# Turning the second norms of batches 1 to 3 by VectorE blocks and memory, in place of TensorE transposes

## What is computed

```
x = x + attention(layernorm(x))     # per batch: 16 heads, gated slot attention with 64 slots
x = x + ffn(layernorm(x))           # the "second norm"
ffn(n) = ((silu(n @ fp8(gate_w) * gate_s) * (n @ fp8(up_w) * up_s)) @ fp8(down_w)) * down_s
```

## Time and profile before

| | |
|---|---|
| median of 3 runs | 1351.48 us (1348.45 to 1352.53) |
| profiled execution, its own time | 1351.25 us |
| its span | 1349.5 us |
| TensorE (PE) busy | 1323.1 us, 98% of the span |
| VectorE (DVE) busy | 1054.4 us, 78% |
| ScalarE (ACT) busy | 426.6 us, 32% |
| granted TensorE clock | 1.00 over the span |
| attention up to the first feed-forward-only step | 0 to about 1097 us |
| feed-forward steps | about 1097 to 1349.5 us |

### The profile page before, as it was taken

How to read it: one execution, slowest core, us unless ns; L and a number is a source line. 1 busy time by engine, 2 the same in 40 slices (tenths; PEclk the granted TensorE clock), 3 DMA queues, 4 the chain that set the end, 5 groups by cost and what they waited for, 6 DMA issues and landing times.

```text
span 1349.5 us, 24276 instructions
## 1 busy us (share of the span) xinstructions
PE 1323.1 (98%) x9287; PEld 1096.6 (81%) x9287; DVE 1054.4 (78%) x1675; ACT 426.6 (32%) x1283; POOL 137.9 (10%) x106
## 2 busy tenths in 40 slices
PE   6999999999999999999999999999999999999998
PEld 5788888788888888888788788878888878888887
DVE  8888888888888888888888888888778875535354
ACT  4333323332333233233323332333333333222221
POOL 3001101110120012001100110111110010000000
PEclk9999999999999999999999999999999999999999
DMA  6147555655665575556655665565333430000000
GB/s 187 40 106 167 123 121 127 163 114 116 147 135 121 115 167 126 126 117 156 132 132 121 152 133 119 118 158 124 87 92 84 124 109 0 32 1 31 0 32 32
DMA packets 500559, 144.58 MB, mean 107 GB/s; under 512 B 359648, under 2 KB 491616, under 8 KB 500448
## 3 DMA queue, kind: packets, MB, share of 16 engines
q1 hardware_dynamic: 500448, 143.08, 45.5%
HBM read 85.80 MB, written 57.21 MB: 106 GB/s over the span
## 4 chain that ended last, share of the span: by engine, by line
PE 78%; DVE 9%; SPq 5%; DMA 4%; issue 2%; ACT 1%; POOL 0%; DVEq 0%
PE bank L486 15%; PE bank L488 14%; PE bank L487 14%; PE bank L118 13%; PE bank L1659 6%; PE bank L726 3%; SPq L369 3%; PE bank L709 2%; PE bank L566 2%; PE bank L546 2%; DMA fp_weights<-q 2%; SPq L334 2%; DMA e_tokens<-k_tok_then_wT 1%; PE bank L645 1%; PE bank L714 1%
## 5 line engine op out<-in xcount | busy, mean ns | idle before, releaser
L486 PE MATMUL bank<-wvg_hi,xT_hi 128*128 128x512 f32 x512 | 206.6, 404 | 0.7
L488 PE MATMUL bank<-wvg_hi,xT_lo 128*128 128x512 f32 x512 | 199.9, 390 | 0.0
L487 PE MATMUL bank<-wvg_lo,xT_hi 128*128 128x512 f32 x512 | 199.7, 390 | 0.0
L786 ACT ACTIVATE a_and_v<-bank 128x256 f32<-128x256 f32 x128 | 49.2, 384 | 326.8 <-PE bank L488 326.8
L486 PEld LDWEIGHTS bank<-wvg_hi,xT_hi 128*128 128x128 f32 x512 | 96.2, 188 | 25.5 <-issue 4.2
L488 PEld LDWEIGHTS bank<-wvg_hi,xT_lo 128*128 128x128 f32 x512 | 96.1, 188 | 20.5
L487 PEld LDWEIGHTS bank<-wvg_lo,xT_hi 128*128 128x128 f32 x512 | 96.3, 188 | 17.8
L1103 DVE RECIPROCAL cT<-cT 128x512 f32<-128x512 f32 x32 | 107.0, 3342 | 0.0
L1048 POOL TENSOR_TENSOR rstd<-ssq,neg_half 128x8 f32<-128x8 f32 x32 | 52.4, 1638 | 490.9 <-DVE ssq L1151 490.9
L486 PE MATMUL bank<-wo_hi,oT_hi 128*128 128x512 f32 x256 | 99.8, 390 | 0.0
L488 PE MATMUL bank<-wo_hi,oT_lo 128*128 128x512 f32 x256 | 99.6, 389 | 0.0
(11 more groups left out here) (168 smaller groups left out, 3036.9 us busy)
## 6 DMA issues: line engine op xcount, KB each, us to landing
o_transposed<-o SPq DMA_DIRECT2D x27, 512.0 KB, 3.4
oT_lo<-o_transposed SPq DMA_DIRECT2D x108, 128.0 KB, 3.0
fp_weights<-q SPq DMA_DIRECT2D x28, 318.0 KB, 3.2
e_tokens<-k_tok_then_wT SPq DMA_DIRECT2D x31, 256.0 KB, 2.3
e_tok<-e_tokens SPq DMA_DIRECT2D x124, 64.0 KB, 2.3
c_tokens<-cT SPq DMA_DIRECT2D x31, 256.0 KB, 2.4
cT<-c_tokens SPq DMA_DIRECT2D x124, 64.0 KB, 2.3
w_slots<-p SPq DMA_DIRECT2D x27, 256.0 KB, 2.4
```

What stands on the lines that cost most here:

```text
L486: pe.matmul(dst, w_hi, m_hi, start=(k == 0), stop=False)
L487: pe.matmul(dst, w_hi, m_lo, start=False, stop=False)
L488: last = pe.matmul(dst, w_lo, m_hi, start=False, stop=(k == n - 1))
L786: return act.activation(dst, src, ACT.Copy)
```

## The change

Batch 0's second norm stays as it was, in unit 29. Batch 1 joins the late ones (LATE = 3, 12 token tiles t = 0 to 11). Its statistics are taken in unit 30 by the late helpers, those of batch 2 in unit 31, those of batch 3 in steps 2 and 3 of batch 1. TensorE no longer turns any late tile. Instead VectorE normalises tile t into half t % 2 of a double buffer, turns its 32x32 blocks in place (late_turn), SyncE stores the tile to DRAM and loads the previous one with the blocks in their places into the other half of the buffer (store_turned, load_turned), ScalarE rounds it into xT_hi and VectorE takes the remainder, both reading SBUF. Tiles 0 to 7 (batches 1 and 2) go through steps 2 to 11 of batch 0; tiles 8 to 11 (batch 3) through steps 4 to 10 of batch 1, after the results of batch 0 have been stored, since they share the buffer. TensorE waits for xT_lo only at step 10 of a batch, ahead of the next batch's first gate product. ScalarE's and VectorE's code for batch 1 is written out, outside of the loop.

```diff
@@ -649 +649 @@
                 if tail and i >= 2:
-                    pe.wait_ge(s_nl, CH * (i - 1))
+                    pe.wait_ge(s_nl, CH)
...
@@ -730 +730 @@
                 return
-            if tail:
-                norm_transposes(i - 1, (0, 1))
+            if tail and i == 1:
+                norm_transposes(0, (0, 1))
             job(VG3, nu, ni)
-            if tail:
-                pe.wait_ge(s_nl, CH * (i - 1) + 2)
-                norm_transposes(i - 1, (2, 3))
+            if tail and i == 1:
+                pe.wait_ge(s_nl, 2)
+                norm_transposes(0, (2, 3))
...
@@ -894 +894 @@
                 copy(e_tok[:, :, :].rearrange("p c m -> p (c m)"), T1[:, :]).then_inc(s_etok, 1)
-            if tail and i >= 2:
-                norm_hi(i - 2, (2, 3))
+            if tail and i == 2:
+                norm_hi(0, (2, 3))
...
@@ -947 +947 @@
             head_squares(u, 0)
-            if tail and not last:
-                norm_hi(i - 1, (0, 1))
+            if tail and i == 1:
+                norm_hi(0, (0, 1))
...
@@ -1063 +1063 @@
             unit((PAIRS - 1) * B + i, i, last=(i == B - 1), tail=True)
-            if i + 1 < B:
-                norm_rsqrt(i - 1, B + i)
+            if i == 1:
+                norm_rsqrt(0, B + 1)
...
@@ -1254 +1254 @@
             nu, ni = u + 1, i + 1
-            if tail and i >= 2:
-                norm_lo(i - 2, (2, 3))
+            if tail and i == 2:
+                norm_lo(0, (2, 3))
...
@@ -1313 +1313 @@
                 add_y(v, 3)
-            if tail and not last:
-                norm_statistics(i - 1)
+            if tail and i == 1:
+                norm_statistics(0)
+            if tail and i == 2:
+                ffn.late_statistics(dve, 0, range(CH))
+                ffn.late_aggregate(dve, 0)
...
@@ -1325 +1328 @@
                 ffn.times_gate(dve, 0, 1)
-                ffn.late_statistics(dve, 0, (0, 1))
+                ffn.late_statistics(dve, 1, (0, 1))
...
@@ -1334 +1337 @@
             c_turn(nu)
-            if tail:
-                norm_tokens(i - 1, (0, 1))
+            if tail and i == 1:
+                norm_tokens(0, (0, 1))
...
             times_gate(u, i, 0)
-            if tail:
-                norm_lo(i - 1, (0, 1))
-                norm_tokens(i - 1, (2, 3))
+            if tail and i == 1:
+                norm_lo(0, (0, 1))
+                norm_tokens(0, (2, 3))
...
@@ -1405 +1408 @@
         mean_square(UNITS - 1)
-        ffn.late_statistics(dve, 0, (2, 3))
-        ffn.late_aggregate(dve, 0)
+        ffn.late_statistics(dve, 1, (2, 3))
+        ffn.late_aggregate(dve, 1)
...
@@ -1421 +1424 @@
 DOWN_GROUPS = ((0, 4), (4, 5), (5, 6), (6, 7), (7, 11), (11, 12))
-LATE = 2
+LATE = 3
...
@@ -1440 +1443 @@
         self.s_var, self.s_sd = sem("late_var_ready"), sem("late_sd_ready")
-        self.s_xn, self.s_xtr = sem("n3_ready"), sem("n3_transposed")
+        self.s_xn, self.s_xb = sem("n3_ready"), sem("n3_blocks_turned")
+        self.s_xst = [sem(f"n3_blocks_stored{n}") for n in range(2)]
+        self.s_xld = [sem(f"n3T_loaded{n}") for n in range(2)]
+        self.n_dram = nc.dram_tensor("second_norms", (LATE * CH, KT, P, P), F32, kind="Internal").ap()
...
@@ -1564 +1570 @@
         tokens(B - 1, last=True)
+    def turned(t):
+        return ffn.xn[:, 2 + t % 2, :].rearrange("p (k t) -> p k t", k=KT)
+    def late_columns(t):
+        at = (B - LATE) * CH + t
+        return slice(at * P, (at + 1) * P)
...
@@ -1625 +1640 @@
         load_down(4)
-        with sp.Fori(0, B) as b:
+        def store_turned(t):
+            sp.wait_ge(ffn.s_xb, t + 1)
+            sp.dma_start(ffn.n_dram[t].rearrange("k p f -> p k f"), ffn.xn[:, t % 2, :].rearrange("p (k f) -> p k f", f=P)
+                         ).then_inc(ffn.s_xst[t % 2], 16)
+        def load_turned(t):
+            sp.wait_ge(ffn.s_xst[t % 2], 16 * (t // 2 + 1))
+            if t >= 2:
+                sp.wait_ge(ffn.s_xl, t - 1)
+            if t >= 2 * CH:
+                sp.wait_ge(ffn.s_out, 16 * CH)
+            for n in range(BL):
+                rows = slice(BK * n, BK * (n + 1))
+                sp.dma_start(ffn.xn[rows, 2 + t % 2, :].rearrange("t (n m) -> t n m", m=BK),
+                             ffn.n_dram[t].rearrange("k (i t) f -> t (k i) f", t=BK)[:, :, rows]
+                             ).then_inc(ffn.s_xld[t % 2], 16)
+        def late_moves(tiles):
+            for t in tiles:
+                store_turned(t)
+                if t > tiles[0]:
+                    load_turned(t - 1)
+            load_turned(tiles[-1])
+        def store_out(b):
...
                              .rearrange("a p d -> (a p) d"), ffn.res[:, c, :]).then_inc(ffn.s_out, 16)
+        late_moves(range(0, 2 * CH))
+        store_out(0)
+        late_moves(range(2 * CH, LATE * CH))
+        with sp.Fori(1, B) as b:
+            store_out(b)
...
     def _(pe):
-        def late_transposes(t, f):
-
-            pe.wait_ge(ffn.s_xn, t + 1)
-            pe.wait_ge(ffn.s_fu, f - 1)
-            for k in range(KT):
-                mm = pe.transpose(ffn.up_bank(f)[:, k * P:(k + 1) * P], ffn.xn[:, t % CH, k * P:(k + 1) * P],
-                                  ffn.ident[:, :])
-            mm.then_inc(ffn.s_xtr, 1)
-
...
@@ -1681 +1717 @@
                     continue
-                late = first and 2 <= f < 2 + LATE * CH
-                if late:
-                    late_transposes(f - 2, f + 2)
+                if f == FT - 2 and not last:
+                    pe.wait_ge(ffn.s_xl, CH if first else LATE * CH)
...
                     ffn.gate_product(pe, b + 1, f + 2 - FT)
-                if late:
-                    pe.wait_ge(ffn.s_xl, f - 1)
...
@@ -1708 +1741 @@
     def _(act):
-        def late_hi(t, f):
-            act.wait_ge(ffn.s_xtr, t + 1)
-            at = (B - LATE) * CH + t
-            act.activation(ffn.xh[:, :, at * P:(at + 1) * P],
-                           ffn.up_bank(f)[:, :].rearrange("p (k t) -> p k t", k=KT), ACT.Copy).then_inc(ffn.s_xh, 1)
-
-        def tokens(b, first=False, last=False):
-            for f in range(FT):
-                if first and f < 4:
-                    continue
+        def late_hi(t):
+            act.wait_ge(ffn.s_xld[t % 2], 16 * BL * (t // 2 + 1))
+            act.activation(ffn.xh[:, :, late_columns(t)], turned(t), ACT.Copy).then_inc(ffn.s_xh, 1)
+        def tokens(b, first=False, second=False):
+            for f in range(4 if first else 0, FT):
...
                 ffn.fuse_hi(act, b, f)
-                if first and f < 3 + LATE * CH:
-                    late_hi(f - 3, f + 1)
+                if first:
+                    late_hi(f - 4)
+                if second and f >= 6 and f < 6 + CH:
+                    late_hi(2 * CH + f - 6)
...
         ffn.fuse_hi(act, 0, 3)
-        late_hi(0, 4)
-        blocks(act, tokens)
+        tokens(0, first=True)
+        tokens(1, second=True)
+        with act.Fori(2, B) as b:
+            tokens(b)
...
@@ -1743 +1776 @@
                 dve.wait_ge(w["out_done"], CH * UNITS)
-            if t >= CH:
-                dve.wait_ge(ffn.s_xtr, t - CH + 1)
-            dve.tensor_scalar(ffn.xn[:, t % CH, :], y[:, (B - LATE) * CH + t, :], ffn.mv[:, t, 0:1],
+            if t == 2 * CH:
+                dve.wait_ge(ffn.s_out, 16 * CH)
+            elif t >= 2:
+                dve.wait_ge(ffn.s_xst[t % 2], 16 * (t // 2))
+            dve.tensor_scalar(ffn.xn[:, t % 2, :], y[:, (B - LATE) * CH + t, :], ffn.mv[:, t, 0:1],
...
-        def late_lo(t, f):
+        def late_turn(t):
+            dve.wait_ge(ffn.s_xn, t + 1)
+            dve.transpose(ffn.xn[:, t % 2, :], ffn.xn[:, t % 2, :]).then_inc(ffn.s_xb, 1)
+        def late_lo(t):
             dve.wait_ge(ffn.s_xh, t + 1)
-            at = (B - LATE) * CH + t
-            cols = slice(at * P, (at + 1) * P)
-            dve.tensor_tensor(ffn.xl[:, :, cols], ffn.up_bank(f)[:, :].rearrange("p (k t) -> p k t", k=KT),
-                              ffn.xh[:, :, cols].bitcast(F32), ALU.subtract).then_inc(ffn.s_xl, 1)
+            cols = late_columns(t)
+            dve.tensor_tensor(ffn.xl[:, :, cols], turned(t), ffn.xh[:, :, cols].bitcast(F32),
+                              ALU.subtract).then_inc(ffn.s_xl, 1)
...
@@ -1779 +1817 @@
-        def tokens(b, first=False, last=False):
+        def tokens(b, first=False, second=False, last=False):
...
                 ffn.times_up(dve, b, f)
-                if first and f < 3 + LATE * CH:
-                    late_lo(f - 3, f + 1)
                 ffn.fuse_lo(dve, b, f)
-                if first and f < 2 + LATE * CH:
+                if first and f > 4:
+                    late_lo(f - 5)
+                if first and f < 2 + 2 * CH:
                     late_norm(f - 2)
-                if first and f == 4:
-                    ffn.late_statistics(dve, 1, range(CH))
-                    ffn.late_aggregate(dve, 1)
+                    late_turn(f - 2)
```

(23 more changed lines are left out.)

## The result

The changed kernel takes 1355.32 us (median of 8 runs, 1352.46 to 1359.37), the kernel before beside it 1350.61 (8 runs, 1348.45 to 1352.53). The ratio is 1.0036, with a 95% interval of 1.0023 to 1.0048: 4.7 us slower, where 6.0 us faster was forecast. The profiled execution took 1356.23 us, its span is 1354.5, 5.0 more than before.

A forecast was written before the change was run, and what follows sets the result against it. TensorE, busy for 98% of the span, was taken as the bound. Feature steps 5.19 plus units 30 and 31 0.79 gave 5.98 us off 1351.25, so 1345.3 us; range 1342.5 to 1349.

The forecast's parts named there:

- so 5.44 each (24 matmuls at 0.227): TensorE's feature steps: a step without transposes takes 5.44 us, so eight in batch 0 take 43.52.
- Feature steps of batch 0, 5.19 us: Steps 2 to 9: removing eight groups of four transposes and a stall in step 4 gains 5.19 us.
- Units 30 and 31, 0.79: Of two groups of eight transposes removed, the one between value products and job VG3 gains 0.79 us.
- The second group of transposes: Behind VG3, before unit 31's gate product: inside TensorE's wait, gains nothing; the wait grows from 0.53 to about 1.4 us.
- Rival (2): Unit 31's start: the drain of VG3 gets shorter too, gaining another 0.79 us, total 1344.5; chance 0.07.
- The added work of VectorE, cost zero: Features: block turns bring a VectorE step to 4.8 of 5.44 us; batch 1's statistics also fit; cost zero.
- The way over memory, cost zero: Batch 0's features: a tile is there 4.7 us after the turn, through store and loads; delays stay within slack.
- the ring: Batch 0's features: turn, store, loads, ScalarE's and VectorE's work to the next turn; 10.7 us per two steps against 10.88.
- (3): Features: part of the gain becomes waits if loads land after 5.4 us, losing 2.7 us: 1348.0; chance 0.13.
- (4): Batch 0's features: the ring exceeds its slack, up to 11.4 us lost, 1356.7, slower; chance 0.03.
- The warning of the Trainium skill that I weighed: Late tiles' DMA: a plain strided transpose is 19 times slower, some 25 us per 128x128 part; forecast used 2.3 us loads.
- chance of 0.04 for slower: Whole kernel: chance 0.04 of being measured slower, against 0.82 for faster and 0.14 for same.

The follow-up runs named there:

- E2: Changed kernel plus 96 unused bytes per partition behind late_sd, its tiles then 256 bytes further than in the kernel before: 1343.28 us, ratio 0.9952.
- E1: Kernel before plus 160 unused bytes per partition behind late_sd, giving the changed kernel's placement: 1361.49 us, ratio 1.0086.
- E9: Kernel before plus 256 unused bytes per partition behind late_sd: 1352.41 us, ratio 1.0001.
- E10: Kernel before plus 128 unused bytes ahead of the first tile, y, so all tiles move together: 1351.54 us, ratio 0.9998.
- E11: Kernel before plus 32 unused bytes ahead of the first tile, y, so all tiles move together: 1353.61 us, ratio 1.0007.
- E3: Changed kernel plus 32 unused bytes behind late_sd, its tiles then 192 bytes further than in the kernel before: 1349.38 us, ratio 0.9992.
- E7: Kernel before with only ws, wk, wq and feature weights 0 to 2 shifted 32 bytes, all behind them 256 bytes: 1355.10 us, ratio 1.0027.
- E8: Kernel before with only wo_hi, wo_lo and down weights 7 to 10 shifted 32 bytes, all else 0 or 256: 1354.10 us, ratio 1.0022.
- E12: Kernel before with only xT_hi and xT_lo shifted 32 bytes, all behind them 256 bytes: 1367.35 us, ratio 1.0105.

## Why the prediction was wrong

**The step that failed** is the one that looked safest: "so 5.44 each (24 matmuls at 0.227)", and with it the whole rest of TensorE's order, which I took as unchanged. It is 5.44 in the kernel before; in the changed one a step takes 5.51 to 5.60. Behind the first down product the features lose, against E2's trace (the changed kernel with matching addresses, 250.8 us there), 3.2 us in 29 gate and up products of features 0 to 2 and 7 to 11 (0.11 each), 0.4 in the 15 of features 3 to 6, and 1.6 in 48 down products (0.03 each): 5.3 us, which eats the gain of 5.2 there (256.0 before, 256.1 after). The attention, whose projections and out products read the same shifted tiles, ends at 1098.4 in place of 1093.5 in the profiles, where 0.8 less was forecast. (Single profiles also differ there by waits for a DMA, line L709: 7.7 us in all before, 5.3 in the changed kernel, 3.7 in E2.) By the medians placement costs 11 us (E1), and the change brings 6: 4.7 us slower. In the sum this cost stood at nothing, without a term of its own. The prediction listed every instruction of the diff, and none of its rivals had an instruction that the diff does not touch. A constant that sizes tiles was in it, and I read it as a count of tiles only. Three small lines of the constructor would have told that all addresses behind move.

**The terms of the sum, read from E2**, where placement is out of the way:

- Feature steps of batch 0, 5.19 us: 43.52 us for eight steps, as worked out, and 250.8 in place of 256.0 for all features. Right.
- Units 30 and 31, 0.79: from the last transposes of unit 29 to the first gate product it is 1022.49 to 1058.95 before and 1019.26 to 1054.84 in E2, 36.46 and 35.58: 0.88, a little more than the term. The second group of transposes lay inside the drain of VG3, as said: the wait grew from 0.53 to 1.41. Rival (2) did not happen.
- The added work of VectorE, cost zero: right. A block turn takes 0.71 us, the remainder from SBUF 0.68. Here is E2's VectorE in batch 1, where the statistics went, and the idle time that is back two steps later, for the earlier trace rows:

```profile
1156.90 2.47 DVE L1553 BATCH_NORM_STATS2 late_stats<-y 128x6 f32<-128x512 f32 x4
...
1166.03 0.71 DVE L1789 STREAM_TRANSPOSE n_then_result<-n_then_result 128x512 f32<-128x512 f32 x1
...
1171.99 0.69 DVE L1532 SCALAR_TENSOR_TENSOR gated<-gated,bank 128x512 f32<-128x512 f32 x1 [1.00 <-ACT gated L1521]
```

- The way over memory, cost zero: right. In E2, store and load land after the times that the nearest rows promised, and ScalarE waits for each of the 12 tiles, 0.4 to 2.6 us; the tanh behind the longer waits follows at once, behind the shorter ones it still has to wait for its gate product:

```profile
second_norms<-n_then_result SPq DMA_DIRECT2D x12, 256.0 KB, 2.4
n_then_result<-second_norms SPq DMA_DIRECT2D x48, 64.0 KB, 2.3
```
```profile
1099.54 0.63 ACT L1747 ACTIVATE xT_hi<-n_then_result 128x512 fp32r<-128x512 f32 x1 [1.20 <-DMA n_then_result<-second_norms]
...
1111.77 0.63 ACT L1747 ACTIVATE xT_hi<-n_then_result 128x512 fp32r<-128x512 f32 x1 [2.56 <-DMA n_then_result<-second_norms]
1112.31 0.67 ACT L1521 ACTIVATE gated<-bank,gate_scale 128x512 f32<-128x512 f32 x1
```

By my count the ring took 10.7 of 10.88 us. In the trace the roundings that follow the longer waits start at 1111.77, 1122.22 and 1132.57, 10.45 and 10.35 us apart: the ring is shorter than two steps and catches up, and no wait of TensorE comes from it. Rivals (3) and (4), the only ones on the slow side, did not take place. The warning of the Trainium skill that I weighed ("VectorE: DVE Perf Modes", section "The three transpose paths") did not bear on these moves: 2.3 us for 64 KB in E2, 2.4 in the changed kernel.

So the chance of 0.04 for slower came from a list of mechanisms inside the change, and the mechanism was outside of it.

## What to carry to other kernels

A change that resizes any allocation moves all that is allocated behind it; compare addresses before comparing instructions, and when the same matmul has another mean duration in the changed kernel, look there first. Keep the tiles that TensorE reads together (the moving one and the weights of the next matmul) at the same start modulo 256 bytes, by a gap if need be: here one unused tile of 96 bytes turned 0.4% slower into 0.5% faster. And a transposition taken off a TensorE that is 98% busy is worth its distance between starts (0.48 us for four), not the sum of its recorded durations.

## What the runs showed of the hardware

- The distance between float32 matmuls of 128x512 depends on where their operands lie relative to each other: 0.227 us where all start at the same place modulo 256 bytes (before, E2, E9, E10, E11), 0.230 to 0.234 in the mean of a product where they don't. By gaps between xT and all that is allocated behind late_sd: 32 bytes 0.6%, 64 bytes 0.5%, 128 bytes 0.5%, 160 bytes 0.9% of the whole kernel; E3's 192 bytes 0.4% against E2.
- The two tiles that count are the one that streams and the one from which the next weights are loaded: in E7 the last matmul of a down product has 0.235 us where the next gate product's weights moved, and 0.227 elsewhere.
- The loss outlasts the mismatch: in E8 and E12 the product behind one takes 1.85 us in place of 1.81.
- The absolute start makes no difference that can be measured (E10 and E11), not even off a multiple of 64 bytes.
- The cause inside the chip is open. The weight load of the next matmul overlaps the reading of the moving operand (1257.65 inside 1257.64 to 1258.04), and it is this pair whose addresses count; whether the two collide in SBUF, or elsewhere, was not measured. Relative shifts above 256 bytes, matmuls of other sizes and other types than float32 were not tried.
